# An attention, MLP and Mamba kernel on one core: the MLP's W2 as float32r products, with the rows of both layer norms scaled by ScalarE

## What is computed

```python
attn_out = out.reshape(B, N, N, E) @ Wo
h = x_in + attn_out
h = _layer_norm(h, ln_agg_g, ln_agg_b)
mlp = jax.nn.relu(h @ W1 + b1) @ W2 + b2
h = mlp + h
return _layer_norm(h, ln_out_g, ln_out_b)
# _layer_norm(x, g, b) = (x - mean) * rsqrt(var + 1e-5) * g + b over the last axis
```

## Time and profile before

| | |
|---|---|
| median of 3 runs | 2421.56 us (2416.81 to 2422.51) |
| the profiled execution, its own time | 2419.65 us |
| its span in the profile | 2417.9 us |
| busy in the span: PE, DVE, ACT, POOL | 86%, 85%, 54%, 51% |
| first times_wo of the MLP; last (chunk 15) | at 1100.14 us; at 1385.83 us |
| first W1 product | at 1124.49 us |
| start of the Mamba block | about 1437 us |
| stretch 1271.90 to 1385.80 us (6 chunks), busy: PE, DVE, ACT, POOL | 113.2, 101.6, 36.8, 0 of 113.9 us |
| TensorE's granted clock in that stretch | 1.00 |

### The profile page before, as it was taken

One profiled execution on the slowest core, in us unless ns is written; L12 is line 12 of the kernel. 1 busy time (PEld: TensorE's weight loads), 2 busy tenths in 40 slices (PEclk: granted clock), 3 DMA queues, 4 the chain that ended last, 5 costly groups with the idle time before them and its releaser, 6 DMA issues. The chain is left out here.

```text
span 2417.9 us, 44041 instructions
## 1 busy us (share of the span) xinstructions
PE 2080.3 (86%) x17272; PEld 1408.8 (58%) x17272; DVE 2059.5 (85%) x2424; ACT 1296.7 (54%) x2834; POOL 1238.8 (51%) x645
## 2 busy tenths in 40 slices
PE   8988977787796676666999978989998999999997
PEld 7867522232242221115788856777777888888886
DVE  4426799999999999995888858999998999999996
ACT  3336677767867774541332335555555555555552
POOL 1102699989999999991110001334333344433434
PEclk9999999999999999998999989999999999999999
DMA  7769312222221213201332224233222234333332
GB/s 235 248 205 251 112 37 54 46 59 54 50 55 20 37 30 65 59 12 30 114 99 79 79 72 75 72 68 80 67 69 71 75 87 98 88 98 101 93 80 62
DMA packets 301359, 204.55 MB, mean 85 GB/s; under 512 B 202080, under 2 KB 279392, under 8 KB 297056
## 3 DMA queue, kind: packets, MB, share of 16 engines
q1 hardware_dynamic: 283120, 147.29, 25.2%
q0 software_dynamic: 8704, 33.56, 3.8%
q10 hardware_dynamic: 9328, 20.88, 3.2%
HBM read 133.76 MB, written 67.90 MB: 83 GB/s over the span
## 5 line engine op out<-in xcount | busy, mean ns | idle before, releaser
L306 DVE TENSOR_TENSOR att_av<-att_att,att_v2ps 128x2816 f32<-128x2816 f32 (+2 forms) x288 | 774.9, 2750 | 20.0 <-PE att_bank L485 17.2
L306 POOL TENSOR_TENSOR att_av<-att_att,att_v2sb 128x1280 f32<-128x1280 f32 x256 | 745.0, 2937 | 36.5 <-PE att_bank L485 32.2
L485 PE MATMUL att_bank<-att_av,att_w 128*32 128x512 f32 x4096 | 535.7, 606 | 220.4 <-DVE att_av L306 201.2
L485 PEld LDWEIGHTS att_bank<-att_av,att_w 128*32 128x32 f32 x4096 | 134.8, 109 | 561.0 <-issue 285.0
L654 ACT ACTIVATE att_ev<-att_bank 128x512 f32<-128x512 f32 x512 | 297.6, 595 | 254.0 <-PE att_bank L485 206.8
L1772 DVE SCALAR_TENSOR_TENSOR mb_cv<-mb_bank,mb_cw,mb_cv 128x504 f32<-128x504 f32 (+2 forms) x480 | 349.4, 733 | 75.1 <-ACT mb_cv L1590 64.6
L1459 PE MATMUL mb_bank<-mb_xT_hi,dt_win_hi 128*128 128x512 f32 x576 | 241.9, 420 | 38.0 <-DVE mb_ms L1816 24.4
L1388 POOL CAST mb_y_hi<-mb_y 128x1024 fp32r<-128x1024 f32 x64 | 67.4, 1054 | 370.1 <-DVE mb_y L1812 370.1
L1393 POOL TENSOR_TENSOR mb_y_lo<-mb_y,mb_y_hi 128x1024 fp32r<-128x1024 f32 x64 | 154.5, 2436 | 181.1 <-DVE mb_S L1781 181.1
L1459 PE MATMUL mb_bank<-mb_xT_lo,dt_win_hi 128*128 128x512 f32 x576 | 232.5, 404 | 0.0
L1459 PE MATMUL mb_bank<-mb_xT_hi,dt_win_lo 128*128 128x512 f32 x576 | 232.0, 403 | 0.0
(11 more groups left out here) (196 smaller groups left out, 3910.3 us busy)
## 6 DMA issues: line engine op xcount, KB each, us to landing
att_xin<-in_x SPq DMA_DIRECT2D x32, 512.0 KB, 4.4
qk_t<-att_qk POOLq DMA_DIRECT2D x16, 1024.0 KB, 5.1
v<-att_vs POOLq DMA_DIRECT2D x16, 1024.0 KB, 5.1
mb_dAb<-dA_rows SPq DMA_DIRECT2D x32, 512.0 KB, 6.3
mb_dAb<-dA_cols SPq DMA_DIRECT2D x32, 512.0 KB, 5.7
mixed_t<-att_ev SPq DMA_DIRECT2D x1020, 8.0 KB
att_q<-qk_t ACTq DMA_DIRECT2D x32, 256.0 KB, 4.7
att_kb<-qk_t ACTq DMA_DIRECT2D x64, 128.0 KB, 3.1
```

Source lines behind the costliest of these rows:

```text
L306: return eng.tensor_tensor(av[t % 2][:, :, d0:d1, :], a.unsqueeze(2).broadcast_to((P, 2, d1 - d0, N)), v2.unsqueeze(1).broadcast_to((P, 2, ...
L485: mm = pe.matmul(bank[r % NB][s * M:(s + 1) * M, :], w[i // WB % 2][:, i % WB, s, :], av[r // 2 % 2][:, i % 2, s * STRIP_D:(s + 1) * STRIP ...
```

## The change

W2 is split on GpSimd at the start, as W1 is. ScalarE makes each hidden tile twice, as float32r (`hid_hi`) and as float32 (`hid`), and GpSimd subtracts one from the other (`hid_lo`, four steps a chunk). W2's product is 48 float32r matmuls in place of 16 float32 ones, in an order in which the low parts come later. In both norms VectorE makes `shift` = -mean · rstd (128x4), ScalarE scales the four token tiles as Identity(x · rstd + shift), and VectorE multiplies by the gain and adds the bias. The second norm's gain and bias of chunk c - 2 (`finish`) and the b2 of chunk c - 1 (`add_b2`) now stand in `front(c)`, between the shift of norm 0 and its gain.

```diff
@@ gpsimd, behind the split of w1
-            for d in range(2):
+            def split_win(d):
                 pool.wait_ge(win_loaded, 16 * d + 16)
...
+            def hid_lo(c):
+                need(pool, w2_done, 2 * c)
+                for i, m in enumerate(ORDER):
+                    pool.wait_ge(hid_ready, FT * c + i + 1)
+                    pool.tensor_tensor(hid_["lo"][:, m, :], hid[:, m, :], hid_["hi"][:, m, :], ALU.subtract)\
+                        .then_inc(hid_lo_ready, 1)
+
+            pool.tensor_copy(w2_["hi"][:, :, :], w2[:, :, :]).then_inc(w2_split, 1)
+            pool.wait_ge(w2_split, 1)
+            pool.tensor_tensor(w2_["lo"][:, :, :], w2[:, :, :], w2_["hi"][:, :, :], ALU.subtract).then_inc(w2_split, 1)
+            for c in range(NCHUNK):
+                hid_lo(c)
+                if c == 5:
+                    split_win(0)
+                if c == 8:
+                    split_win(1)
@@ tensor, mlp
-                for t in range(TT):
-                    for i, k in enumerate(ORDER):
-                        if t == 0:
-                            pe.wait_ge(hid_ready, FT * c + i + 1)
-                        mm = pe.matmul(OUT_[t // 2][:, (t % 2) * E:(t % 2 + 1) * E], hid[:, k, t * P:(t + 1) * P],
-                                       w2[:, k, :], start=(i == 0), stop=(i == FT - 1))
-                    if t % 2:
-                        mm.then_inc(w2_done, 1)
-                    if t == 2:
-                        turn_h(c + 1, 1 - u)
+                times_w2(c, 0, "hi")
+                times_w2(c, 2, "hi")
+                times_w2(c, 0, "lo")
+                times_w2(c, 1, "hi")
+                times_w2(c, 1, "lo").then_inc(w2_done, 1)
+                times_w2(c, 2, "lo")
+                turn_h(c + 1, 1 - u)
+                times_w2(c, 3, "hi")
+                times_w2(c, 3, "lo").then_inc(w2_done, 1)
+
+            def times_w2(c, t, part):
+                for i, k in enumerate(ORDER):
+                    if t == 0:
+                        pe.wait_ge(hid_hi_ready if part == "hi" else hid_lo_ready, FT * c + i + 1)
+                    for wn in ("hi", "lo") if part == "hi" else ("hi",):
+                        mm = pe.matmul(OUT_[t // 2][:, (t % 2) * E:(t % 2 + 1) * E], hid_[part][:, k, t * P:(t + 1) * P],
+                                       w2_[wn][:, k, :], start=(part == "hi" and i == 0 and wn == "hi"),
+                                       stop=(part == "lo" and i == FT - 1))
+                return mm
@@ tensor, before the loop
+            pe.wait_ge(w2_split, 2)
@@ scalar
+            def scale_rows(n, c, v, out):
+                act.wait_ge(shifted[n], c + 1)
+                if n == 1:
+                    need(act, o_stored[c % 2], c // 2 * 16)
+                    need(act, x1_turned, 2 * (c - 1))
+                for t in range(TT):
+                    act.activation(out[:, t, :], v[:, t, :], ACT.Identity, bias=shift[n][:, t:t + 1],
+                                   scale=rstd[n][:, t:t + 1]).then_inc(scaled[n], 1)
...
                     act.wait_ge(hid_done, FT * c + i + 1)
+                    act.activation(hid_["hi"][:, m, :], HID_[m][:, :], ACT.Relu, bias=b1[:, m:m + 1]).then_inc(hid_hi_ready, 1)
                     act.activation(hid[:, m, :], HID_[m][:, :], ACT.Relu, bias=b1[:, m:m + 1]).then_inc(hid_ready, 1)
...
                 relu(c, c % 2)
                 if c + 1 < NCHUNK:
+                    scale_rows(0, c + 1, h[1 - c % 2], h[1 - c % 2])
                     copy_hT(c + 1, 1 - c % 2)
                 root(1, c)
+                scale_rows(1, c, hb[c % 2], o[c % 2])
@@ vector, norm_of_rows (was layer_norm) and gain_and_bias
                 chain.link(dve.reciprocal(rstd[n][:, :], std[n][:, :]))
-                for t in range(TT):
-                    ins = dve.tensor_scalar(out[:, t, :], v[:, t, :], mv[n][:, t, 0:1], rstd[n][:, t:t + 1],
-                                            ALU.subtract, ALU.mult)
-                chain.link(ins)
+                dve.scalar_tensor_tensor(out=shift[n][:, :], in0=mv[n][:, :, 0], scalar=-1.0, in1=rstd[n][:, :],
+                                         op0=ALU.mult, op1=ALU.mult).then_inc(shifted[n], 1)
+            def gain_and_bias(n, c, chain, out, gain, bias, done):
+                dve.wait_ge(scaled[n], TT * c + TT)
                 chain.link(dve.tensor_tensor(out[:, :, :], out[:, :, :], wide(gain), ALU.mult))
                 dve.tensor_tensor(out[:, :, :], out[:, :, :], wide(bias), ALU.add).then_inc(done, 1)
@@ vector, front and back
-                layer_norm(0, c, chain, h[u], h[u], row["g1"], row["be1"], h_ready)
-                dve.wait_ge(h_ready, c + 1)
+                norm_of_rows(0, c, chain, h[u])
+                if c >= 2:
+                    finish(c - 2)
+                if c >= 1:
+                    add_b2(c - 1)
+                gain_and_bias(0, c, chain, h[u], row["g1"], row["be1"], h_ready)
...
-                dve.tensor_tensor(hb[u][:, :, :], h[u][:, :, :], wide(row["b2"]), ALU.add).then_inc(b2_added, 1)
+                if c == NCHUNK - 1:
+                    finish(c - 1)
+                    add_b2(c)
...
-                need(dve, o_stored[u], (c // 2) * 16)
-                need(dve, x1_turned, 2 * (c - 1))
-                layer_norm(1, c, chain, hb[u], o[u], row["g2"], row["be2"], o_ready)
+                norm_of_rows(1, c, chain, hb[u])
@@ vector, behind the loop
+            finish(NCHUNK - 1)
```

More of the change, by code:

```diff
@@ L802, in block_mlp @@
         hT = {n: [sb(f"hT{u}_{n}", [P, KT, CHUNK], F32R) for u in range(2)] for n in ("hi", "lo")}
-        w1_ = {n: sb(f"w1_{n}", [P, KT, F], F32R) for n in ("hi", "lo")}
+        w1_, w2_ = [{n: sb(f"{w}_{n}", shape, F32R) for n in ("hi", "lo")}
+                    for w, shape in (("w1", [P, KT, F]), ("w2", [P, FT, E]))]
         hid = sb("hid", [P, FT, CHUNK])
+        hid_ = {n: sb(f"hid_{n}", [P, FT, CHUNK], F32R) for n in ("hi", "lo")}
         o = [sb(f"o{u}", [P, TT, E]) for u in range(2)]
@@ L809, in block_mlp @@
         rstd = [sb(f"rstd{n}", [P, TT]) for n in range(2)]
+        shift = [sb(f"shift{n}", [P, TT]) for n in range(2)]
         wdt = sb("wdt", [P, KT, 32])
@@ L819, in block_mlp @@
         h_ready, h_turned, hT_hi_ready, hT_lo_ready = sem("h_ready"), sem("h_turned"), sem("hT_hi_ready"), sem("hT_lo_ready")
-        w1_split = sem("w1_split")
+        w1_split, w2_split, hid_hi_ready, hid_lo_ready = (sem("w1_split"), sem("w2_split"), sem("hid_hi_ready"),
+                                                          sem("hid_lo_ready"))
+        shifted, scaled = [sem(f"shifted{n}") for n in range(2)], [sem(f"scaled{n}") for n in range(2)]
         hid_done, hid_ready, w2_done, w2_added = sem("hid_done"), sem("hid_ready"), sem("w2_done"), sem("w2_added")
@@ L832, in block_mlp @@
         ln_ready, r_ready, prod_ready = sem("ln_ready"), sem("r_ready"), sem("prod_ready")
-        LINKS = (4, 4)
+        LINKS = (3, 3)
         rows_in = x.rearrange("(c t p) e -> c p t e", t=TT, p=P)
@@ L890, in _ @@
                         .then_inc(win_split, 1)
-                pool.wait_ge(win_split, 2 * KT * d + 2 * KT)
+            def hid_lo(c):
[13 more added lines that the diff above has]
+                    split_win(1)
         @block.tensor
@@ L1036, in _ @@
             root(0, 0)
+            scale_rows(0, 0, h[0], h[0])
             copy_hT(0, 0)
@@ L1068, in wide, with norm_of_rows @@
                 return v[:, :].unsqueeze(1).broadcast_to((P, TT, E))
-            def layer_norm(n, c, chain, v, out, gain, bias, done):
+            def norm_of_rows(n, c, chain, v):
                 for t in range(TT):
@@ L1081, in layer_norm, with finish, add_b2 @@
                 chain.link(dve.reciprocal(rstd[n][:, :], std[n][:, :]))
-                for t in range(TT):
-                    ins = dve.tensor_scalar(out[:, t, :], v[:, t, :], mv[n][:, t, 0:1], rstd[n][:, t:t + 1],
-                                            ALU.subtract, ALU.mult)
-                chain.link(ins)
+                dve.scalar_tensor_tensor(out=shift[n][:, :], in0=mv[n][:, :, 0], scalar=-1.0, in1=rstd[n][:, :],
+                                         op0=ALU.mult, op1=ALU.mult).then_inc(shifted[n], 1)
+            def gain_and_bias(n, c, chain, out, gain, bias, done):
+                dve.wait_ge(scaled[n], TT * c + TT)
                 chain.link(dve.tensor_tensor(out[:, :, :], out[:, :, :], wide(gain), ALU.mult))
                 dve.tensor_tensor(out[:, :, :], out[:, :, :], wide(bias), ALU.add).then_inc(done, 1)
+            def finish(c):
+                gain_and_bias(1, c, Chain(dve, b_chain, c * LINKS[1] + LINKS[1] - 1), o[c % 2], row["g2"], row["be2"], o_ready)
+            def add_b2(c):
+                dve.wait_ge(h_ready, c + 1)
+                dve.tensor_tensor(hb[c % 2][:, :, :], h[c % 2][:, :, :], wide(row["b2"]), ALU.add).then_inc(b2_added, 1)
             def front(c, u):
```

## The result

| | before | after |
|---|---|---|
| median, us (range, runs) | 2420.67 (2416.81 to 2422.51, 4) | 2491.16 (2487.68 to 2494.10, 4) |
| span of the profiled execution | 2417.9 | 2490.1 |
| first `times_wo` to the Mamba block's first instruction (1437.23 before, 1511.12 after) | 337.1 | 412.1 |
| 12 intervals of `times_wo`, fourth start to sixteenth | 229.1 | 287.9 |
| mean granted clock of TensorE, 1446.4 to 1511 (before: 1385.8 to 1437.2) | 0.90 | 0.80 |

The ratio is 1.0293 (95% interval 1.0277 to 1.0309): **70.5 us slower**, where 46 were forecast and the range ended at 2488. All of it lies in the MLP: 75 us between the two marks, against 72 in the span. Of the 75, 3.0 lie ahead of the fourth start of `times_wo`, 58.8 in the 12 intervals and 13.3 behind the last start.

The account below looks back on a forecast made before the run. TensorE bound at 18.72 us a chunk, VectorE 1 us behind; h would come late, period about 21.5. 12 times 2.8 = 33.6, plus 2.5, 3, 2.8 and 4, made +46: 2468 us, range 2437 to 2488.

Parts of the forecast that it names:

- TensorE's own work, 17.6 a chunk, worth nothing: W2's float32r matmuls cut TensorE's work by 1.1 to 17.6 us a chunk, but it waits for h.
- The root behind the second tile; reciprocal at t = 10.0: Norm 0's root waits in ScalarE's queue, so the reciprocal is hardly earlier than 10.9; period 19.6 to 19.7 us.
- GpSimd and VectorE take turns, +2.0: `hid_lo` subtractions hold up VectorE's shift and two of five 128x1024 steps: 2.0 us a chunk, period about 21.5.
- Nothing to spare; the cost is hidden.: SyncE's queue: `xin`, behind the later store, lands at 21.5, just when `times_wo` wants it, at no cost.
- rival C: Late loads: transfers take 8 us for 6.5, period 22.8 to 23, +15 to 20, 2486 us; chance 0.14.
- The two splits ..., and ScalarE's table loads come in a fuller queue: +3.: Mamba's weight splits on GpSimd meet VectorE's five steps, and table loads meet a fuller ScalarE queue: +3 us in all.
- The tail, +6.8: After the last `times_wo`: 2.8 us for chunk 14, and +4 for chunk 15's `finish(14)`, b2, `hid_lo` wait and `finish(15)`.
- Rival A: No contention to speak of between GpSimd and VectorE: 19.65 us per chunk, +20, 2441 us; chance 0.17.
- Rival B: TensorE binds at 17.6 us a chunk, 2405 us; the change wins if the root comes below t = 7.8; chance 0.06.
- beside the first three of the five: ScalarE's scalings of h lie beside the first three of VectorE's five 128x1024 gain, bias and b2 steps.
- Rival D: TensorE's clock falls to 1.2 GHz behind waits of about 1.5 us; near 2495 us; chance 0.04.

Follow-up runs that it names:

- W2 part without the subtraction: The kernel before with only W2's new product and split, norms still on VectorE, GpSimd's four `hid_lo` subtractions left out, low products reading `hid_hi`: 2421.44 us.
- early loads: The changed kernel with the loads of the chunk after issued one store earlier, so that none stands behind a store in SyncE's queue: 2484.70 us.
- norms' part alone: The changed kernel with only its norm changes: `hid` made once, the old W2 loop, no `hid_lo`: 2463.64 us (ratio 1.0182).

## Why the prediction was wrong

The sign held, and so did the mechanism of the clean chunk: slower, because h comes later than TensorE needs it. The size did not: 24.5 us are missing from the sum, most of them in terms that I had walked past, the table loads and the late loads.

- **TensorE's own work, 17.6 a chunk, worth nothing.** The 17.6 was half a microsecond short: TensorE is busy 18.11 a chunk in the W2 part without the subtraction. That it is worth nothing is right, and for a stronger reason than I gave: VectorE's own chunk without GpSimd was 18.65.
- **The root behind the second tile; reciprocal at t = 10.0.** Right in kind, 10.40 in the clean chunk (early loads, 1361.04). 0.4 of it is TensorE's wait for x1T, which I had booked at 0.2 and then taken off again as overlapped. A scaling takes 0.50 from start to start where I took 0.42, at my upper bound, so the copies of x1T start at t = 5.29 and not at 4.9.
- **GpSimd and VectorE take turns, +2.0.** From reciprocal to the end of h I had 8.7; it is 8.89 (1361.04 to 1369.93). The two long steps lose 0.97 and 1.06, where I took 0.85; the shift 0.56, where I took 0.3; the rest of the stretch, 6.3, was 0.4 shorter than my 6.7. The Trainium skill, page SBUF — State Buffer, section Who interferes with whom, has the two block each other in full; the 1.06 lies between its reading (1.24) and mine. Leaving `hid_lo` out gave 1.63 a chunk, as the scalings then bind. **The clean period is 22.10 for 21.5: 0.6 times 12 is 7 us missing.**
- **"Nothing to spare; the cost is hidden."** Wrong. xin landed late in seven chunks of 1180 to 1440, by up to 3.51 us; the clock fell behind two of these waits, 3.51 and 2.15, and not behind 2.59 and 2.01. In the chunk of the rows the store goes out at t = 15.15 where I had 14.1 and `xin` at 16.1, and the load of a Mamba weight in the same queue, which I had left out, makes the two longest waits. It is 6.5 us by experiment, 9.5 between the 12 intervals of the two traces. Late loads, which I had only as rival C and as an alternative to the sum, run on top of it at a third of C's price. C's slower transfers are a part of it: from issue to landing `xin` took 7.0 in the median, where it had taken 6.5, and 8.3 in the chunk of the rows.
- **"The two splits ..., and ScalarE's table loads come in a fuller queue: +3."** This is the step that failed. I sized it at 3. Moving the table loads alone gave 11.2 us, and the two split chunks are then still 2.8 and 3.3 over the clean one. I had seen the fuller queue and not walked it: x1T waits behind the load, TensorE behind x1T, the second tile behind that, and the reload stands ahead of the root that everything waits for.
- **The tail, +6.8.** 13.3 in the trace (64.7 for 51.4 behind the last start), 7.9 once the tables are moved (59.3). The tail itself was sized right, but in part for another cause: in the norms' part alone it falls from 56.7 to 52.6 with the copies of x1T ahead of the scalings, a wait that my sum did not have.
- **The sum again,** by the traces, forecast in brackets: 3.0 (2.5) ahead of the fourth start; clean chunks 12 times 3.38, 40.6 (33.6); long chunks 8.7 (3), which is 13.2 less the 4.5 that before has over clean ones; late loads 9.5 (0); behind the last start 13.3 (6.8), of which 4.7 go with the table loads. Together 75.1 (45.9). So the table loads with the splits are missed by some 10, the loads by 9.5 (6.5 by the times) and the clean period by 7.
- **Rival A** (no contention) fell with L1143 at 2216 ns. **Rival B** fell too, and its deciding point with it: with the root early, the reciprocal came at t = 7.94, next to the 7.8 that I had named, and the period was 20.89, not 17.6. The turns with GpSimd stayed, and the scalings behind the fourth tile were a wall that I had called "beside the first three of the five".
- **Rival D.** I wrote that waits as short as these are borne. Those of 1.2 to 1.4 were (1.00 over 1399 to 1446), and so were 2.59 at 1281.47 and 2.01 at 1377.26; behind 2.15 the clock fell, and behind 2.06 it fell with early loads (1239.14) but not in the changed kernel (1237.22). The length of the last wait alone does not decide it, and I can't say what does. The Trainium skill, page TensorE: Matmul & The Clock Gate, Part 1, has idling gate the clock and work release it; the trace agrees behind the wait of 2.15, with 0.61 and 0.54, and 1.00 again from 1356.

## What to carry to other kernels

When work is moved to an engine with time to spare, its queue is in order: walk the whole queue of a chunk, the rare entries (a table load, a weight split) above all, and ask of each later instruction who waits for it. Behind a wait that was moved there is often a second one almost as long, here the root, GpSimd's turns and the scalings of h: taking away the first or the second gave periods of 20.89 and 20.47 for 22.10, and then the scalings bound. So one edit wins less than its own wait, and the gains don't add. And before an engine's work is shortened, see whether another one's own chunk is as long: VectorE's 18.65 beside TensorE's 18.72 left W2 nothing to win.

## What the runs showed of the hardware

- Four 128x256 Identity activations with scale and bias from SBUF take 2.07 to 2.08 us, 0.50 from start to start and 587 ns or so each, where the plain 128x256 one took 417 ns.
- A `TENSOR_TENSOR` of VectorE in SBUF lost 0.97 to 1.06 us to one GpSimd subtraction of 1.29, and the two subtractions beside these took 4.28 (at 1339.69) in place of 2.58. Readers of PSUM lost nothing (means of 687 to 689 ns; nine of the 96 had GpSimd beside them for over half of their time, at 677 to 692). A shift of 128x4 (0.16 alone) took up to 1.05 beside one.
- TensorE's granted clock stayed at 1.00 through waits of 1.2 to 1.4 us, and in the same run through one of 2.59, and fell to 0.54, near the lower level of 1.2 GHz, after one of 2.15, for some 4 us.
- A table load is issued ahead of its activation's wait: Sqrt's at 1223.59 began 3.4 us before its root started, and ScalarE still waited 2.16 for the moments behind it, so this reload cost nothing.
